# Last projection with the weights stationary, attention output in channel rows, and a new order of steps

## The chip, the cores and the metric

The kernel runs on one core of a Trainium2 chip. A core has a matrix engine (TensorE), three engines for elementwise work (VectorE, ScalarE, GpSimd), and SyncE, which here issues all DMAs. Each engine runs its own instruction list in order and waits on semaphores for the others. The metric is the device time of one execution in microseconds, median of several runs.

## The reference, cut to what matters

The input x has 4 sequences (batches) of 512 tokens with 256 channels. Two layers are computed, each followed by a residual addition and a layer norm.

```python
mixed = silu(causal_conv(x @ w_qkv, conv_w))     # 16 key heads, 32 value heads, 128 wide
q, k = l2norm(q) * 128 ** -0.5, l2norm(k)        # each key head serves two value heads
beta, g = sigmoid(x @ w_b), -exp(A_log) * softplus(x @ w_a + dt_bias)
def step(state, (q_t, k_t, v_t, g_t, b_t)):      # 512 tokens in sequence
    state = state * exp(g_t)
    delta = (v_t - k_t @ state) * b_t
    state = state + outer(k_t, delta)
    return state, q_t @ state
o = rmsnorm(o * silu(x @ w_z)) * norm_gamma      # per head
x = layernorm(x + o.reshape(..., 4096) @ w_out)  # the last projection of the attention
x = layernorm(x + moe(rmsnorm(x)))               # 8 experts, the top 2 of them weighed, and a shared one
```

All of it is float32.

## The kernel before

A body is one key head (two value heads) of one batch: 16 x 4 = 64 bodies. The recurrence is done in four chunks of 128 tokens, so a body has 8 cells (chunk x value head) of 128 x 128. In each cell a triangular matrix has to be inverted. That goes by doubling: six levels of `join` (a product with the blocks found so far), a mask on VectorE (`join` there, giving N), `growx` on TensorE, a copy to X on ScalarE (`growx` there), and a DMA that turns X into XT (`flip`). `growx` of a level needs the `flip` of the level before. After level 5, `newton`, `res`, `finish` and `tt` refine the inverse. The other steps of a body are: `proj` and `gate` (input projections, two or four matmuls each), `tap`, `conv`, `silu` (the convolution), `ktp`, `squares`, `kraw` (norms), `products`, `m`, `p`, `scan`, `diag` (decays and products of keys), then for the four chunks in sequence `read` (state times keys), `rhs`, `solve`, `u`, `write` and `s` (the new state, S), and `out`. `og` multiplies by the gate, `power`, `pow`, `ogs` norm the result.

The result then has to change its layout for the last projection: `ot` (L1386 to L1389) transposes 32 x 32 blocks on VectorE, `ost` (L871) writes them to DRAM and `old` (L838) loads them back as ogT with the channels on the partitions. `project` (L1156 to L1166) multiplies with wo, `acc` (L1400) adds the product to acc, which holds 128 token rows of 256 channels for each tile, over all heads. wo is w_out times gamma, scaled by GpSimd (`scale_wo`, L900 to L906) right behind `ogs`. `vt`, `vst`, `vld` do the same exchange of layout for v.

The order of all this is written out by hand in the table ORDER. Each engine has a list of (step, index, ahead); `rounds` runs it once per round k, for body k + ahead, so a round holds the work of four bodies at different ages. SP's list (L843 to L882) issues the DMAs: `flip`, `x0`, `vst`, `vld`, `ost`, `old`, `egs` and `ecs` (512 KB each, a row of decay factors spread over all partitions), and `weights`, once in four rounds (w_kh 768 KB, and wo_raw 256 KB, which waits for s_wog, that is for the scaling of the previous head's wo).

The expert layer runs at the end over four batches of 9 experts: `into` (L565) and `outof` (L581) on TensorE. For each batch `prepare_*` (L518 to L721) computes in numbered parts: part 0 adds acc to the rows of x (L670) and takes the statistics of the norm, part 2 normalises, parts 3 to 6 are the second norm, part 7 (L596) transposes, part 8 (L602) multiplies for the router, part 10 weighs. The parts of batch 0 stand in the functions `drain` of each engine, among the last bodies; those of batch 1 in part there, the rest between the experts.

Of the kernel before, what the change touches and what calls it, by code (L numbers as in the profile page):

```python
# [1494 lines left out]
```

## Time and profile before

| | us |
|---|---|
| three runs | 2419.18, 2420.91, 2423.63 |
| the profiled execution | 2420.51 |
| its span | 2418.8 |
| TensorE busy | 2197.0 |
| VectorE busy | 1900.1 |
| ScalarE, GpSimd busy | 1211.4, 1174.0 |

The span is the time from the first to the last instruction of the profiled execution. Busy time of TensorE is the sum over matmuls that overlap in a pipeline, so a stretch that is 100% busy can still be one in which matmuls start late; the distance between two starts is the better measure. An f32 matmul is two instructions in the records. In a timeline a row merges equal neighbours ("x8"), and what stands in brackets is the idle time ahead of it and who ended it.

### The profile page before, as it was taken

Reading aid. Unit: us, or ns where it says so; the run is one execution under the profiler, and the core shown is the slowest. Engines: PE = TensorE matmul, PEld = TensorE weight load, DVE = VectorE, ACT = ScalarE, POOL = GpSimd, SP = SyncE. Lnnn points to the kernel's source line nnn. Section 1 sums busy time; section 2 is a strip of 40 time slices with the busy share of each in tenths; the row PEclk is TensorE's granted clock in tenths of the full one; section 3 lists DMA queues with packets and bytes.
Section 4 is the critical chain, followed back from the end, with each engine's and each line's share of the span. In section 5 each row is a group of like instructions: output and inputs, shape, how many; then the busy total and the mean of one; then the engine's idle time right before and its main releaser. Section 6 shows DMA issues by size and latency. Waiting matters only on the chain.

```text
span 2418.8 us, 48563 instructions
## 1 busy us (share of the span) xinstructions
PE 2197.0 (91%) x16974; PEld 1709.1 (71%) x16974; DVE 1900.1 (79%) x3299; ACT 1211.4 (50%) x3805; POOL 1174.0 (49%) x1194
## 2 busy tenths in 40 slices
PE   6889999998999999998999999999998999978998
PEld 3677777776777777777777777777777777755565
DVE  4778888887888888787888888888888888864666
ACT  3555555554555555555555555555555555531210
POOL 2445555545554555554555545555554655531000
PEclk8999999999999999999999999999999999988999
DMA  3666767676767677577777676776767686662000
GB/s 117 156 146 159 177 151 164 148 167 153 165 149 162 153 161 173 145 167 149 166 158 171 141 166 152 166 171 156 165 142 166 158 176 145 147 151 69 27 9 18
DMA packets 597346, 349.88 MB, mean 145 GB/s; under 512 B 487665, under 2 KB 558705, under 8 KB 596849
## 3 DMA queue, kind: packets, MB, share of 16 engines
q1 hardware_dynamic: 597104, 346.78, 63.0%
q8 instruction: 137, 2.24, 0.4%
q14 instruction: 105, 0.85, 0.1%
HBM read 159.50 MB, written 69.73 MB: 95 GB/s over the span
## 4 chain that ended last, share of the span: by engine, by line
PE 46%; DMA 27%; DVE 13%; issue 5%; SPq 3%; ACT 2%; POOL 0%; POOLq 0%; DVEq 0%; ACTq 0%
DMA XT<-X 19%; PE bank L1034 9%; PE bank L1163 6%; DMA o_blocks<-og 6%; DVE og L1388 5%; PE bank L565 5%; PE bank L1053 4%; PE bank L1153 4%; DVE conv L1320 4%; PE bank L1087 3%; PE bank L1152 3%; PE bank L581 2%; SPq L838 2%; PE bank L1126 2%; DMA ogT<-o_blocks 2%
## 5 line engine op out<-in xcount | busy, mean ns | idle before, releaser
L1320 DVE SCALAR_TENSOR_TENSOR conv<-bank,cw_all,conv 128x511 f32<-128x511 f32 (+2 forms) x768 | 572.5, 746 | 20.6 <-ACT conv L1212 6.9
L1034 PE MATMUL bank<-xT,w_kh 128*128 128x512 f32 x1024 | 534.8, 614 | 1.6 <-ACT kraw L1241 1.1
L1265 ACT ACTIVATE X<-bank 128x512 f16<-128x512 f32 x384 | 228.6, 595 | 531.5 <-PE bank L1087 531.4
L1163 PE MATMUL bank<-wo,ogT 128*128 128x256 f32 x1024 | 287.3, 425 | 20.3 <-DMA ogT<-o_blocks 20.0
L987 POOL TENSOR_TENSOR ms<-ms,epsq 128x8 f32<-128x8 f32 x64 | 12.7, 198 | 584.8 <-ACT og L1278 584.8
L1163 PEld LDWEIGHTS bank<-wo,ogT 128*128 128x128 f32 x1024 | 256.6, 334 | 34.6 <-DMA ogT<-o_blocks 23.4
L1053 PE MATMUL bank<-w_kh,xT 128*128 128x256 f32 x1024 | 269.0, 396 | 4.7 <-DVE conv L1320 4.7
L1212 ACT ACTIVATE conv<-bank,cw_all 128x512 f32<-128x512 f32 x256 | 175.9, 687 | 162.1 <-PE bank L1034 162.1
L1077 PEld LDWEIGHTS bank<-X,mhiT 128*128 128x128 f16 x3072 | 145.6, 99 | 135.0 <-issue 75.4
L1087 PE MATMUL bank<-N,XT 128*128 128x64 f16 x2560 | 127.9, 193 | 119.8 <-DMA XT<-X 117.8
L1346 DVE TENSOR_TENSOR N<-bank,lev 128x512 f16<-128x512 f32 x320 | 218.0, 681 | 21.6 <-PE bank L1077 19.0
L1400 DVE TENSOR_TENSOR acc<-bank,acc 128x512 f32<-128x512 f32 x128 | 88.4, 692 | 182.2 <-PE bank L1163 182.2
L963 POOL TENSOR_SCALAR_AFFINE_SELECT mhiT<-m32T 128x512 f16<-128x512 f32 x128 | 78.8, 637 | 309.9 <-DVE m32T L1332 309.9
L1087 PEld LDWEIGHTS bank<-N,XT 128*128 128x128 f16 x2560 | 102.6, 98 | 153.3 <-issue 143.0
L1034 PEld LDWEIGHTS bank<-xT,w_kh 128*128 128x128 f32 x1024 | 170.2, 191 | 42.8 <-issue 31.6
L1053 PEld LDWEIGHTS bank<-w_kh,xT 128*128 128x128 f32 x1024 | 183.3, 194 | 23.4 <-DVE conv L1320 5.9
L1235 ACT ACTIVATE sqj<-bank 128x128 f16<-128x128 f32 x512 | 134.4, 277 | 124.8 <-PE bank L1044 124.8
L1153 PE MATMUL bank<-U,pT 128*128 128x128 f32 x1024 | 192.9, 280 | 0.0
L1136 PEld LDWEIGHTS bank<-U,keys 128*128 128x128 f32 x768 | 111.0, 192 | 83.2 <-ACT U L1270 65.1
L1356 DVE TENSOR_TENSOR TT<-bank,XT 128x512 f32<-128x512 f32 x128 | 82.5, 686 | 102.1 <-PE bank L1109 102.1
L1077 PE MATMUL bank<-X,mhiT 128*128 128x64 f16 x3072 | 154.8, 194 | 4.9 <-DMA X<-XT 2.9
L1152 PE MATMUL bank<-S,qE 128*128 128x128 f32 x768 | 153.6, 282 | 0.0
(176 smaller groups left out, 5088.0 us busy)
## 6 DMA issues: line engine op xcount, KB each, us to landing
egb<-rows SPq DMA_DIRECT2D x64, 512.0 KB, 4.7
ecb<-rows SPq DMA_DIRECT2D x64, 512.0 KB, 5.0
v_blocks<-conv SPq DMA_DIRECT2D x64, 512.0 KB, 3.0
vT<-v_blocks SPq DMA_DIRECT2D x256, 128.0 KB, 3.1
o_blocks<-og SPq DMA_DIRECT2D x64, 512.0 KB, 3.8
ogT<-o_blocks SPq DMA_DIRECT2D x256, 128.0 KB, 3.0
...
```

The source lines that it names most:

```text
L1034: mm = pe.matmul(PB[j % 2][:, :], w[:, k, g * P:(g + 1) * P], xT[:, k, b * SEQ:(b + 1) * SEQ], start=(k == 0), stop=(k == KT - 1))
L1053: mm = pe.matmul(PB[h][:, 256 * c:256 * c + 256], xT[:, k, t * P:(t + 1) * P], w[:, k, 512:768], start=(k == 0), stop=(k == KT - 1))
L1077: mm = pe.matmul(IB[p][:, x * 64:(x + 1) * 64], mhiT[:, p, x, :], blocks(X[:, p, x:x + 1, :], i, 0), start=True, stop=True)
L1087: mm = pe.matmul(IB[p][:, x * 64:(x + 1) * 64], XT[:, p, x, :], (last_N[:, x, :] if i == 5 else N[:, p, x, :]), start=True, stop=True)
L1152: pe.matmul(dst, qE[:, p, x, :], S[:, c, v * P:(v + 1) * P], start=True, stop=False)
L1153: mm = pe.matmul(dst, pT[:, p, x, :], U[:, x, :], start=(c == 0), stop=True)
L1163: mm = pe.matmul(OB[h][:, 256 * c:256 * c + 256], flat(ogT)[:, 2 * i + v::CELLS], wo[:, head % 2, v, :], start=(v == 0), stop=(v == VH - 1))
L1212: act.activation(conv[:, g, :], PB[i % 2][:, :], ACT.Copy, scale=cw_all[:, head, g * TAPS + 3:g * TAPS + 4]).then_inc(s_tap, 1)
L1235: act.activation(sqj[:, i, c, :], PB[i][:, c * P:(c + 1) * P], ACT.Square, accum_out=ssum[:, p, i, c:c + 1]).then_inc(s_sq, 1)
L1265: act.activation(blocks(X[:, p], i, 0), packed(IB[p], i), ACT.Copy).then_inc(s_x[p], 1)
L1320: dve.scalar_tensor_tensor(conv[:, g, m:], PB[j % 2][:, 0:SEQ - m], cw_all[:, head, g * TAPS + 3 - m:g * TAPS + 4 - m], conv[:, g, m:], op ...
L1346: dve.tensor_tensor(N[:, p].rearrange("p x (b s) -> p x b s", s=LEVELS[i]), packed(IB[p], i), blocks(lev[:, 1 + i:2 + i, :], i, 0).broadca ...
```

## The change

Four things change together.

The last projection: before, each of four chunks multiplied the tokens of a chunk (stationary, every eighth element) with wo (moving, 256 columns), for two value heads. Now wo is stationary (128 of its 256 output channels) and all 512 tokens of the body move, so that a body has four matmuls of 512 columns. The product has output channels on the partitions. acc is kept in this layout, 2 x 128 channel rows by 2048 tokens.

The exchange of layout: `ot` writes its blocks in the order that `vt` uses, and ogT is read in runs of 32 tokens.

The first norm: since acc is in channel rows, a new part 0 on TensorE transposes it by eight 128 x 128 blocks for each batch into two PSUM banks, and part 0 on VectorE adds x in two instructions from PSUM. For batch 0 the transposes stand behind `write` 1 of the last body but one; for the others ahead of or between the experts. Parts 0 and 2 of batch 1 on VectorE move from behind the last `ot` to behind the first expert steps.

The order: all five lists of ORDER are new.

```diff
 ORDER = {
     "tensor": [
-        ("join", 5, 1), ("out", 0, 0), ("solve", 3, 0), ("out", 1, 0), ("out", 2, 0), ("growx", 5, 1), ("out", 3, 0),
-        ("gate", 2, 2), ("join", 0, 2), ("newton", 0, 1), ("newton", 1, 1), ("growx", 0, 2), ("gate", 3, 2),
-        ("proj", 0, 3), ("join", 1, 2), ("finish", 0, 1), ("finish", 1, 1), ("proj", 1, 3), ("proj", 2, 3),
-        ("solve", 0, 1), ("growx", 1, 2), ("proj", 3, 3), ("write", 0, 1), ("products", 1, 2), ("join", 2, 2),
-        ("ktp", 0, 3), ("read", 1, 1), ("ktp", 1, 3), ("products", 0, 3), ("solve", 1, 1), ("growx", 2, 2),
-        ("write", 1, 1), ("proj", 4, 3), ("ktp", 2, 3), ("ktp", 3, 3), ("read", 2, 1), ("proj", 5, 3), ("join", 3, 2),
-        ("solve", 2, 1), ("proj", 6, 3), ("write", 2, 1), ("growx", 3, 2), ("proj", 7, 3), ("join", 4, 2),
-        ("gate", 0, 3), ("gate", 1, 3), ("read", 3, 1), ("project", 0, 0), ("project", 1, 0), ("growx", 4, 2),
-        ("project", 2, 0), ("project", 3, 0),
+        ("proj", 0, 3), ("join", 1, 2), ("finish", 0, 1), ("proj", 1, 3), ("finish", 1, 1), ("growx", 1, 2),
+        ("proj", 2, 3), ("solve", 0, 1), ("proj", 3, 3), ("write", 0, 1), ("join", 2, 2), ("read", 1, 1),
+        ("ktp", 0, 3), ("ktp", 1, 3), ("products", 1, 2), ("growx", 2, 2), ("solve", 1, 1), ("proj", 4, 3),
+        ("write", 1, 1), ("proj", 5, 3), ("join", 3, 2), ("ktp", 2, 3), ("read", 2, 1), ("ktp", 3, 3),
+        ("products", 0, 3), ("solve", 2, 1), ("growx", 3, 2), ("proj", 6, 3), ("write", 2, 1), ("join", 4, 2),
+        ("proj", 7, 3), ("gate", 0, 3), ("gate", 1, 3), ("project", 0, 0), ("growx", 4, 2), ("project", 1, 0),
+        ("project", 2, 0), ("join", 5, 2), ("project", 3, 0), ("read", 3, 1), ("out", 0, 1), ("out", 1, 1),
+        ("solve", 3, 1), ("out", 2, 1), ("growx", 5, 2), ("join", 0, 3), ("out", 3, 1), ("growx", 0, 3),
+        ("newton", 0, 2), ("newton", 1, 2), ("gate", 2, 3), ("gate", 3, 3),
     ],
     "vector": [
...
-        ("tt", 0, 2), ("tt", 1, 2), ("join", 1, 3), ("conv", 0, 4), ("conv", 1, 4), ("conv", 2, 4), ("s", 0, 2),
-        ("conv", 3, 4), ("conv", 4, 4), ("rhs", 1, 2), ("join", 2, 3), ("conv", 5, 4), ("ot", 0, 1), ("s", 1, 2),
...
+        ("join", 1, 2), ("tt", 0, 1), ("tt", 1, 1), ("conv", 0, 3), ("conv", 1, 3), ("conv", 2, 3), ("s", 0, 1),
+        ("join", 2, 2), ("conv", 3, 3), ("rhs", 1, 1), ("ot", 0, 0), ("conv", 4, 3), ("conv", 5, 3), ("p", 0, 2),
...
     "pool": [
-        ("diag", 0, 2), ("mhi", 0, 2), ("mhi", 1, 2), ("pairs", 0, 2), ("qe", 0, 1), ("pow", 0, 0), ("ogs", 0, 0),
-        ("ogs", 1, 0), ("keys", 0, 2), ("eq", 0, 2), ("mlo", 0, 2), ("kn", 0, 3),
+        ("pow", 0, 0), ("ogs", 0, 0), ("ogs", 1, 0), ("eq", 0, 2), ("kn", 0, 3), ("diag", 0, 3), ("mhi", 0, 3),
+        ("mhi", 1, 3), ("pairs", 0, 3), ("mlo", 0, 3), ("keys", 0, 3), ("qe", 0, 2),
     ],
     "sync": [
-        ("flip", 5, 1), ("flip", 0, 2), ("vst", 0, 2), ("flip", 1, 2), ("vld", 0, 2), ("egs", 0, 4), ("ost", 0, 0),
-        ("flip", 2, 2), ("old", 0, 0), ("ecs", 0, 3), ("flip", 3, 2), ("flip", 4, 2), ("x0", 0, 3), ("weights", 0, 2),
+        ("ecs", 0, 2), ("weights", 0, 4), ("flip", 1, 2), ("vld", 0, 2), ("ost", 0, 0), ("flip", 2, 2), ("egs", 0, 4),
+        ("old", 0, 0), ("flip", 3, 2), ("flip", 4, 2), ("x0", 0, 3), ("flip", 5, 2), ("flip", 0, 3), ("vst", 0, 3),
     ],
 }
...
-        acc = sb("acc", [P, TILES, D])
+        acc = sb("acc", [P, KT, TILES * P])
...
-        ogT4 = flat(ogT).rearrange("p (a k) -> p a k", a=Q32)
+        vn, ogT4 = quarters(vT), quarters(ogT)
...
         def prepare_tensor(pe, k, g):
+            if k == 0:
+                if g == 0:
+                    pe.wait_ge(s_zs, 2 * BODIES)
+                    pe.wait_ge(s_acc, 2 * (BODIES - B + 1))
+                elif g == 1:
+                    pe.wait_ge(s_acc, 2 * BODIES)
+                else:
+                    pe.wait_ge(s_rt, (g - 1) * RT + 1)
+                for c in range(CH):
+                    for t in range(KT):
+                        mm = pe.transpose(PICKS[g][c // 2][:, 256 * (c % 2) + P * t:256 * (c % 2) + P * (t + 1)],
+                                          acc[:, t, (g * CH + c) * P:(g * CH + c + 1) * P], ident)
+                mm.then_inc(s_atp, 1)
...
         def moe_tensor(pe):
+            prepare_tensor(pe, 0, 1)
             for i in range(DRAINED, B * NX):
...
+                if 0 < g < B - 1 and e == 0:
+                    prepare_tensor(pe, 0, g + 1)
...
         def prepare_vector(dve, k, g):
-                dve.tensor_tensor(xg[g], xg[g], acc[:, g * CH:(g + 1) * CH, :], ALU.add).then_inc(s_x1, 1)
+                dve.wait_ge(s_atp, g + 1)
+                for j in range(2):
+                    part = xg[g][:, 2 * j:2 * j + 2]
+                    dve.tensor_tensor(part, PICKS[g][j][:, :].rearrange("p (c n) -> p c n", c=2), part, ALU.add).then_inc(s_x1, 1)
...
                 elif name == "project":
-                    for v in range(VH):
-                        mm = pe.matmul(OB[h][:, 256 * c:256 * c + 256], flat(ogT)[:, 2 * i + v::CELLS], wo[:, head % 2, v, :],
-                                       start=(v == 0), stop=(v == VH - 1))
+                    mm = pe.matmul(OB[h][:, :], wo[:, head % 2, v, h * P:(h + 1) * P],
+                                   ogT4[:, :, v::VH].rearrange("p a c r -> p c a r"), start=(v == 0), stop=(v == VH - 1))
...
                 elif name == "ot":
-                    dve.transpose(flat(og2).rearrange("p (b s x) -> p b x s", b=Q32, x=CELLS),
+                    dve.transpose(flat(og2).rearrange("p (b x s) -> p b x s", b=Q32, s=32),
...
-                elif (name, i, n) == ("ot", 0, BODIES - 1):
-                    prepare_vector(dve, 0, 1)
-                    prepare_vector(dve, 2, 1)
```

ScalarE's list moves `growx` 0 ahead of `power` 0 and `zs`, `kraw` to right behind `squares` 0, and the copy for `join` 5 to behind `vals` and one `silu`.

## Rows read from the trace of the kernel before

**Rows 1.** The page's head and its part 1: busy time of each engine.
```profile
span 2418.8 us, 48563 instructions
...
PE 2197.0 (91%) x16974; PEld 1709.1 (71%) x16974; DVE 1900.1 (79%) x3299; ACT 1211.4 (50%) x3805; POOL 1174.0 (49%) x1194
```

**Rows 2.** The view by windows, 60 rounds: stretch, its length, busy times, granted clock.
```profile
112.32:2106.53 1994.21, 1840.73 (x15241) 1474.75 (x15240) 1647.92 (x2700) 1092.83 (x3482) 1080.65 (x1095) 1.00 0.71 159
```

**Rows 3.** Part 5 of the page, groups by line: busy, mean ns, idle before.
```profile
L1034 PE MATMUL bank<-xT,w_kh 128*128 128x512 f32 x1024 | 534.8, 614 | 1.6 <-ACT kraw L1241 1.1
...
L1163 PEld LDWEIGHTS bank<-wo,ogT 128*128 128x128 f32 x1024 | 256.6, 334 | 34.6 <-DMA ogT<-o_blocks 23.4
...
L1034 PEld LDWEIGHTS bank<-xT,w_kh 128*128 128x128 f32 x1024 | 170.2, 191 | 42.8 <-issue 31.6
```

**Rows 4.** Groups by line of TensorE over the whole span, the same columns.
```profile
L1077 PE MATMUL bank<-X,mhiT 128*128 128x64 f16 x3072 | 154.8, 194 | 4.9 <-DMA X<-XT 2.9 <-ACT X L1265 2.1
...
L1087 PE MATMUL bank<-N,XT 128*128 128x64 f16 x2560 | 127.9, 193 | 119.8 <-DMA XT<-X 117.8 <-DVE N L1346 1.6
```

**Rows 5.** TensorE's timeline of one round: start, length, step; L1087 is growx.
```profile
1202.99 2.27 PE L1163 MATMUL bank<-wo,ogT 128*128 128x256 f32 x8
1205.09 0.40 PE L1077 MATMUL bank<-X,mhiT 128*128 128x64 f16 x8
...
1208.09 0.40 PE L1087 MATMUL bank<-last_N,XT 128*128 128x64 f16 x8
...
1211.35 0.41 PE L1087 MATMUL bank<-N,XT 128*128 128x64 f16 x8
...
1214.08 1.94 PE L1034 MATMUL bank<-xT,w_kh 128*128 128x512 f32 x4
1215.85 0.61 PE L1126 MATMUL bank<-vals,TT 128*128 128x128 f32 x4
1216.30 0.40 PE L1087 MATMUL bank<-N,XT 128*128 128x64 f16 x8
...
1219.29 0.60 PE L1114 MATMUL bank<-S,kT 128*128 128x256 f32 x2
...
1221.28 0.40 PE L1087 MATMUL bank<-N,XT 128*128 128x64 f16 x8
...
1228.79 0.39 PE L1087 MATMUL bank<-N,XT 128*128 128x64 f16 x8 [0.93 <-DMA XT<-X]
...
1235.28 0.39 PE L1087 MATMUL bank<-N,XT 128*128 128x64 f16 x8 [0.78 <-DMA XT<-X]
```

**Rows 6.** VectorE's timeline of the same round: vt, the copy of S, ot.
```profile
1208.73 1.25 DVE L1392 STREAM_TRANSPOSE conv<-vT 128x1024 f32<-128x1024 f32 x1 [0.65 <-ACT vT L1226]
...
1218.15 0.48 DVE L1374 COPY S<-bank 128x128 f32<-128x128 f32 x2
...
1221.75 2.06 DVE L1388 STREAM_TRANSPOSE og<-og 128x1024 f32<-128x1024 f32 x1
```

**Rows 7.** SP's timeline of the same round: ost, flip 2, ecs, flip 3.
```profile
1223.84 0.34 SPq L871 DMA_DIRECT2D o_blocks<-og  x1
1224.22 1.96 SPq L856 DMA_TRANSPOSE XT<-X  x1
...
1229.40 0.43 SPq L841 DMA_DIRECT2D ecb<-rows  x1
1229.87 1.24 SPq L856 DMA_TRANSPOSE XT<-X  x1
```

**Rows 8.** GpSimd's timeline of the same round: the scaling of wo.
```profile
1217.63 1.04 POOL L905 TENSOR_TENSOR wo<-wo_raw,gam 128x512 f32<-128x512 f32 x1
```

**Rows 9.** Part 6 of the page, DMA issues: size, median us from issue to landing.
```profile
ecb<-rows SPq DMA_DIRECT2D x64, 512.0 KB, 5.0
```

**Rows 10.** TensorE's timeline in the tail: the last body's newton.
```profile
2176.70 0.27 PE L1099 MATMUL bank<-X,mhiT 128*128 128x128 f16 x1 [7.63 <-POOL mloT L971]
```

**Rows 11.** The chain that ended last, in order of time: the transposes of one batch.
```profile
2340.33 0.87 PE bank L596 x8
```

More of the change, by code:

```diff
@@ L46 @@
-        ("silu", 3, 2), ("growx", 5, 1), ("power", 0, 0), ("zs", 0, 2), ("growx", 0, 2), ("power", 1, 0),
-        ("zs", 1, 2), ("tap", 0, 3),
+        ("zs", 1, 1), ("tap", 0, 2), ("growx", 1, 1), ("u", 0, 0), ("tap", 1, 2), ("silu", 0, 2), ("squares", 0, 2),
+        ("kraw", 0, 2), ("growx", 2, 1), ("u", 1, 0), ("silu", 1, 2), ("tap", 2, 2), ("squares", 1, 2), ("u", 2, 0),
+        ("growx", 3, 1), ("tap", 3, 2), ("growx", 4, 1), ("vals", 0, 1), ("vals", 1, 1), ("silu", 2, 2),
+        ("join", 5, 1), ("u", 3, 0), ("silu", 3, 2), ("growx", 5, 1), ("growx", 0, 2), ("power", 0, 0), ("zs", 0, 2),
@@ L48 @@
+        ("power", 1, 0),
     ],
     "vector": [
-        ("m", 0, 3), ("m", 1, 3), ("acc", 0, 0), ("rhs", 3, 1), ("conv", 9, 3), ("acc", 1, 0), ("conv", 10, 3),
-        ("conv", 11, 3), ("og", 0, 1), ("vt", 0, 3), ("og", 1, 1), ("join", 0, 3), ("res", 0, 2), ("res", 1, 2),
-        ("tt", 0, 2), ("tt", 1, 2), ("join", 1, 3), ("conv", 0, 4), ("conv", 1, 4), ("conv", 2, 4), ("s", 0, 2),
-        ("conv", 3, 4), ("conv", 4, 4), ("rhs", 1, 2), ("join", 2, 3), ("conv", 5, 4), ("ot", 0, 1), ("s", 1, 2),
@@ L54 @@
-        ("p", 0, 3), ("rhs", 2, 2), ("p", 1, 3), ("join", 3, 3), ("conv", 6, 4), ("conv", 7, 4), ("conv", 8, 4),
-        ("s", 2, 2), ("scan", 0, 4), ("scan", 1, 4), ("join", 4, 3),
+        ("join", 1, 2), ("tt", 0, 1), ("tt", 1, 1), ("conv", 0, 3), ("conv", 1, 3), ("conv", 2, 3), ("s", 0, 1),
+        ("join", 2, 2), ("conv", 3, 3), ("rhs", 1, 1), ("ot", 0, 0), ("conv", 4, 3), ("conv", 5, 3), ("p", 0, 2),
+        ("s", 1, 1), ("p", 1, 2), ("join", 3, 2), ("rhs", 2, 1), ("conv", 6, 3), ("conv", 7, 3), ("scan", 0, 3),
@@ L56 @@
+        ("conv", 8, 3), ("m", 0, 3), ("scan", 1, 3), ("join", 4, 2), ("m", 1, 3), ("conv", 9, 3), ("conv", 10, 3),
+        ("s", 2, 1), ("acc", 0, 0), ("rhs", 3, 1), ("acc", 1, 0), ("conv", 11, 3), ("og", 0, 1), ("join", 0, 3),
+        ("vt", 0, 3), ("og", 1, 1), ("res", 0, 2), ("res", 1, 2),
     ],
     "pool": [
-        ("diag", 0, 2), ("mhi", 0, 2), ("mhi", 1, 2), ("pairs", 0, 2), ("qe", 0, 1), ("pow", 0, 0), ("ogs", 0, 0),
-        ("ogs", 1, 0), ("keys", 0, 2), ("eq", 0, 2), ("mlo", 0, 2), ("kn", 0, 3),
+        ("pow", 0, 0), ("ogs", 0, 0), ("ogs", 1, 0), ("eq", 0, 2), ("kn", 0, 3), ("diag", 0, 3), ("mhi", 0, 3),
@@ L238, in build_kernel @@
         s_xg = sem("s_xg")
+        s_atp = sem("s_atp")
         s_x1 = sem("s_x1")
@@ L503, in rows @@
                     sp.wait_ge(s_qe, BODIES - 1)
-                    sp.wait_ge(s_x1, 1)
+                    sp.wait_ge(s_x1, 2)
                 else:
@@ L761, in moe_vector @@
                     g, e = divmod(i, NX)
+                    if i == DRAINED:
+                        prepare_vector(dve, 0, 1)
+                        prepare_vector(dve, 2, 1)
                     if g + 1 < B:
@@ L892, in _ @@
             pool.memset(row_t[0][:, :, 0:1], 0.0).then_inc(s_rowz, 1)
-            pool.memset(acc[:, :, :], 0.0).then_inc(s_zero, 1)
+            pool.memset(flat(acc), 0.0).then_inc(s_zero, 1)
             for i, v in enumerate((0.5, -1.0)):
@@ L1396, in run @@
                     b = n % B
-                    a = acc[:, b * CH + 2 * i:b * CH + 2 * i + 2, :]
+                    a = acc[:, i, b * SEQ:(b + 1) * SEQ]
                     if n < B:
                         dve.wait_ge(s_zero, 1)
-                    dve.tensor_tensor(a, OB[i][:, :].rearrange("p (c n) -> p c n", c=2), a, ALU.add).then_inc(s_acc, 1)
+                    dve.tensor_tensor(a, OB[i][:, :], a, ALU.add).then_inc(s_acc, 1)
             def drain(name, i, n):
```

20 lines of the change are left out of this document (9 added, 11 removed).

## The prediction, made before the change was run

> **What bounds the kernel now.** I read the page's head and part 1 first: span 2418.8 us, TensorE busy 91% [rows 1]. The profiled execution took 2420.51 us, 1.7 more than its span and 0.4 under the median of 2420.91, so a change of the span carries over to the median one to one. The view by windows then shows the body loop: from the first full round to the last it takes 1994.21 us for 60 rounds, 33.24 us each, at a granted clock of 1.00, the 2.4 GHz level [rows 2]. Everything else is 425 us of start and tail. So the loop is the place.
>
> Busy TensorE is not full TensorE here. In the groups by line [rows 4] `growx` (L1087) is the one group with a large idle time ahead of it, 119.8 us, nearly all of it waiting for the DMA that turns X (`flip`). The TensorE timeline of one round [rows 5] shows where. I name the six growx steps of a body g0 to g5. Distances of starts: g5 to g0 3.26 us, g0 to g1 4.95, g1 to g2 4.98, g2 to g3 7.51, g3 to g4 6.49, and g4 to g5 5.33 (0.23 for g4 itself, then 1202.99 to 1208.09). A step's price is the distance to the next start in this timeline. With it the steps inside the first, second, third and last of these need 3.2, 4.9, 4.9 and 5.3 us, so TensorE is full there. The other two hold 5.35 and 5.7 us of work, and are long because flip 2 and flip 3 land late. In all 29.3 us of the mean round are work and 3.9 are stalls. This round has 32.5 us; the longer ones wait longer for the same two flips.
>
> Why flip 2 is late stands in SP's queue [rows 7]. SP issues in order, and `ost` stands ahead of flip 2 and waits for VectorE's transpose `ot`, which runs from 1221.75 to 1223.81 [rows 6]; so flip 2 goes out at 1224.22, 2.94 us after g2 starts, and g3 starts 4.57 us later. Flip 3 follows the 512 KB broadcast `ecs` at 1229.40 and g4 waits for it.
>
> **The projection.** Before: 8 matmuls of 256 columns with the tokens stationary, 16 instructions; eight start within 2.10 us, 4.20 us a round [rows 5]. After: 4 matmuls of 512 columns, 8 instructions of the form of L1034 [rows 3], four of which take 1.77 us (1214.08 to 1215.85), 3.54 us in all [rows 5]. Saved 0.66 us a round. The same columns are multiplied; what goes is half the loads. The old load takes 334 ns against 191 for one read in a row [rows 3], because its columns are 8 elements apart; the new one reads `wo` in a row. The new moving operand is read in runs of 32 elements. No row has that in f32. The nearest is `join` (L1077), whose moving f16 operand lies in runs of 2 to 64: 194 ns against 193 for growx with its operand in a row [rows 4]. So I price the runs at nothing. Upper end: the factor 334/191 on the whole matmul, 0.775 us each, 6.2 us a round, 2.0 more than now. A gain from the runs is excluded: L1034 reads in a row already.
>
> The Trainium skill ("SBUF — State Buffer", Door 1: The DMA port swizzle) says that SBUF serves accesses in 16-byte lines, so that f32 can be strided for free only within 4 elements. The trace agrees for the old load, 334 against 191 ns at a stride of 8. By that rule the runs of 32, eight full lines each, cost nothing either, and the sum stays; the upper end above would need a cost of another kind.
>
> **VectorE.** `ot` wrote with a stride of 8 and takes 2.06 us; it now has the form of `vt`, 1.25 us [rows 6]. That saves 0.8 us a round on VectorE, whose idle time is about 5 us in this round; alone it is worth nothing, but `ost` and flip 2 hang on it. `acc` keeps its shape. The four block loads keep their 1 KB runs: nothing.
>
> **The new order.** I walked the new lists through one round with the old durations. Steps between two growx change as follows (price per step: proj 0.885, project 0.885, gate 0.91, solve or write 0.45, read 0.44, products 0.90, newton pair 0.90, out 0.90, join 0.23).
> - g0 to g1: newton and gate 2 come in, proj 2 and solve 0 go out: 4.95+0.90+0.91-0.885-0.45 = 5.4 us. Flip 0 goes out about 1.1 after g0, behind flip 5, and needs some 4: hidden.
> - g1 to g2: proj 2 and solve 0 in, one products and solve 1 out: 4.97. Here is a new wait: read 1 now comes straight after write 0 and join 2, but needs VectorE's copy of S, which takes 0.48 us and starts some 0.2 after write 0 ends (the copy at 1218.15, the read at 1219.29 [rows 5, 6]); before, products hid it. Stall 0.5, so 5.5. Behind read 1 stand ktp, products, growx 2 and all later TensorE work, and on VectorE rhs 1 and then ot.
> - g2 to g3: 5.4 us of work, but flip 2 still decides. On VectorE `ot` moves ahead of conv 5 (0.7) and ends 0.8 sooner, against tt put in front: by my walk it ends about 1.8 after g2 instead of 2.5, and flip 2 goes out at about 2.2. The way from there to g3 was 4.57 in this round; `egs` no longer lies ahead, but the block loads of v are close. I keep 4.5: 6.7 us.
> - g3 to g4: proj 6, write 2 in, read 3 and half the project work out: 5.4 of work. `ecs` (5.0 us to land [rows 9]) is gone from ahead of flip 3, so its way should fall from the 6.49 seen to about 5.6.
> - g4 to g5: 6.3 of work, with read 3, project 3 and the first outs; nothing late.
> - g5 to g0: join 0 and the last out, 1.4; N must be ready 0.9 after join 0, just as long as VectorE needs (0.68 and the way). 1.5.
> Sum 31.0 us. What moved into the light work elsewhere: `ecs` now lies ahead of flip 1. Flip 1 goes out about 4 after ecs does and has 4 us to land, so in ordinary rounds I count 0.1: 31.1.
>
> Once in four rounds SP has `weights` ahead of flip 1. Its second DMA waits for the previous scaling of `wo` on GpSimd (L905, 1.04 us, right behind ogs, ending at 1218.67, 7.3 us after g0 [rows 5, 8]); in the old order this lay two rounds back, in the new one it is the scaling of the same round, while flip 1 would go out some 6.5 after g0. So flip 1, the loads of v and all that SP has behind them go out about 2 us later, and 1 MB more lies in the DMA queue ahead. TensorE waits about 3 us at g2, of which g2 to g3 gives 1 back, since ost is then ready earlier. 2 us in 4 rounds: 0.5 a round. The bounds are 0 and 1.2 (5 us in four).
>
> Round 31.6 against 33.24: 1.64 saved, 61 rounds, 100 us.
>
> **Start and tail.** GpSimd now makes mlo and keys a step earlier. In the tail TensorE stands 7.6 us at the last newton, waiting for mlo behind a norm step [rows 10]; that goes, and the flips or the X copy are late about 1 us instead: -6.5. Added: 32 transposes to turn the attention rows, 8 for each batch at 0.87 us like L596 [rows 11], 3.5 us, of which the last three batches lie on a TensorE that is full there; and the norm of batch 1 (4.6 us of VectorE) now stands between two experts instead of in VectorE's idle time, up to 2 us. The last project saves 0.7. Net -2, between -8 and +5. The start I leave at 0, plus or minus 5. Four batches of two PSUM additions instead of one SBUF addition: 0.2 us each, hidden.
>
> **Sum.** 2418.8 - 100 - 2 = 2317 for the span; with 1.7 around it 2318, and 0.4 more for the median of runs.
>
> **Rivals.**
> - TensorE alone decides. If both flips arrive in time, a round is 28.7 us of work and 0.8 of small waits, 29.5: 61 x 3.7 = 226 us less, 2193. For it: ot earlier, ecs away from flip 3. Against it: flip 2 still needs ot, ost and its own way after g2, 6.7 us against 5.4 of work.
> - The stalls only move. Then 0.66 us a round is left, less the 0.5 for weights or so: 10 to 40 us, 2380 to 2410. For it: ecs and weights now ahead of flip 1, and the read right behind the write. Against it: g2 to g3 loses its 0.7 on VectorE by rows.
> - Slower: the moving operand in runs costs what the strided load does. Each instruction 0.775 us, 2.0 us a round more than now; of the 1.64 above 0.98 are the order's, so the round is 34.3 and the time 2480. It decides from 0.65 us an instruction on ((4.20+0.98)/8), and if the stalls only move, from 0.53 (4.20/8). For it: the load at a stride of 8. Against it: the row of join.
> - Changed roles without effect (the loop does not feel it, within 0.2%, 5 us): hardly, the project work lies on a TensorE that is full in four of six gaps.
>
> **How the numbers follow.** Forecast 0.56; TensorE alone 0.15 (with the space between, 2200 to 2270); the stalls only move 0.19; no change 0.03; slower 0.07. 0.2% is about what a measurement of this kernel tells from no change. Faster 0.90, same 0.03, slower 0.07. The forecast's own range is 2275 to 2355; taking in half of each neighbour gives 2235 to 2385.
>
> **What would show it.** L1163 has 512 instructions, four starting within 1.77 us; three or more says that the runs cost. The transpose og<-og takes 1.25. g3 waits about 1.3 for flip 2, g4 at most 0.3. The S copy releases L1114 with about 0.5 at read 1. Every fourth round is 2 us longer, with g2 waiting for a flip behind w_kh. No wait for mloT of 7 us at the last newton. The forecast is wrong if the mean round is outside 31.0 to 32.3, above all if g2 waits in every round, which would mean that ecs ahead of flip 1 was underpriced.

## The result, and the profile after

| | before | after |
|---|---|---|
| median of four runs, us | 2420.05 | 2318.30 |
| lowest to highest | 2416.37 to 2423.63 | 2314.64 to 2323.43 |
| span of the profiled execution | 2418.8 | 2316.6 |

The ratio is 0.9581, 95% interval 0.9558 to 0.9605: 102 us faster. The forecast was 2318.

The page's head, its part 1 and two groups of its part 5 after the change (part 5: busy us, mean ns of one | idle before, releaser):

```profile
span 2316.6 us, 47612 instructions
...
PE 2153.8 (93%) x16494; PEld 1561.7 (67%) x16494; DVE 1843.2 (80%) x3303; ACT 1198.6 (52%) x3805; POOL 1224.3 (53%) x1194
...
L1184 PE MATMUL bank<-ogT,wo 128*128 128x512 f32 x512 | 268.3, 628 | 24.4 <-DMA ogT<-o_blocks 23.9
...
L1109 PE MATMUL bank<-N,XT 128*128 128x64 f16 x2560 | 127.7, 194 | 51.3 <-DMA XT<-X 49.1
```

TensorE's own work fell by 43 us [rows 1]. All its idle time, span less busy, fell from 221.8 [rows 1] to 162.8 us: 59 of the 102 us are stalls that went. The idle time ahead of `growx` (now L1109) fell from 119.8 [rows 4] to 51.3 us; other waits grew, as shown below. The view by windows over 60 rounds of the changed kernel (stretch, length, busy times, granted clock, DMA share, GB/s):

```profile
114.02:2006.52 1892.50, 1795.89 (x14761) 1333.07 (x14761) 1592.34 (x2700) 1080.80 (x3482) 1127.99 (x1095) 0.99 0.78 167
```

31.54 us a round against 33.24 [rows 2], so the loop gave 101.7 of the 102.2 us of span. The DMA share rose from 0.71 to 0.78. The same bytes in less time make about 0.75 of it; the rest is that the packets took some 4% longer in all.

TensorE's timeline of an ordinary round after (start, length, step):

```profile
1213.97 0.40 PE L1109 MATMUL bank<-N,XT 128*128 128x64 f16 x8
...
1219.86 0.40 PE L1109 MATMUL bank<-N,XT 128*128 128x64 f16 x8
...
1223.52 0.70 PE L1136 MATMUL bank<-S,kT 128*128 128x256 f32 x2 [0.35 <-DVE S L1397]
...
1225.39 0.40 PE L1109 MATMUL bank<-N,XT 128*128 128x64 f16 x8
...
1231.23 0.40 PE L1109 MATMUL bank<-N,XT 128*128 128x64 f16 x8
...
1236.95 0.40 PE L1109 MATMUL bank<-N,XT 128*128 128x64 f16 x8
1237.18 1.96 PE L1184 MATMUL bank<-ogT,wo 128*128 128x512 f32 x4
1238.98 0.40 PE L1099 MATMUL bank<-X,mhiT 128*128 128x64 f16 x8
...
1243.26 0.40 PE L1109 MATMUL bank<-last_N,XT 128*128 128x64 f16 x8
```

The growx rows (L1109) are g0 to g5. Four project instructions start within 1.80 us (1237.18 to 1238.98); before, eight took 2.10 [rows 5]. No growx waits for a flip here, and so it is in most ordinary rounds (those without `weights`): of the 41 between 250 and 2000 us, g3 waits in 14, for 0.21 us in the mean of all, and g4 in none. VectorE's and SP's timelines of the same round:

```profile
1225.15 1.23 DVE L1411 STREAM_TRANSPOSE og<-og 128x1024 f32<-128x1024 f32 x1
```

```profile
1226.42 0.34 SPq L893 DMA_DIRECT2D o_blocks<-og  x1
1226.84 1.51 SPq L878 DMA_TRANSPOSE XT<-X  x1
1228.39 0.77 SPq L863 DMA_DIRECT2D egb<-rows  x1
```

`ot` takes 1.23 instead of 2.06 us [rows 6] and starts before g2. Flip 2 goes out at 1226.84, 1.45 us after g2 instead of 2.94 [rows 5, 7]. g3 starts 4.39 us behind it, but no longer because of it: TensorE's own steps fill the gap.

Every fourth round, with `weights`, looks different. SP, GpSimd and TensorE in such a round:

```profile
1153.18 0.43 SPq L863 DMA_DIRECT2D ecb<-rows  x1
1153.71 0.77 SPq L841 DMA_DIRECT2D w_kh<-w_heads  x1
1159.05 0.33 SPq L844 DMA_DIRECT2D wo_raw<-w_out  x1
1159.42 1.24 SPq L878 DMA_TRANSPOSE XT<-X  x1
```

```profile
1157.98 1.04 POOL L927 TENSOR_TENSOR wo<-wo_raw,gam 128x512 f32<-128x512 f32 x1
```

```profile
1155.43 0.40 PE L1109 MATMUL bank<-N,XT 128*128 128x64 f16 x8
1163.38 0.39 PE L1109 MATMUL bank<-N,XT 128*128 128x64 f16 x8 [2.25 <-DMA XT<-X]
...
1164.20 1.92 PE L1056 MATMUL bank<-xT,w_kh 128*128 128x512 f32 x2
```

SP stands at wo_raw from 1154.5 until the scaling of wo ends at 1159.02; flip 1 goes out behind it, and g2 comes 7.95 us after g1 instead of 5.53. Rounds of this kind take 33.7 us in the mean (32.6 to 34.7), the others 30.9 (29.9 to 31.9).

The stall at g2 has a second price. The two `proj` instructions at 1164.20 take 1.71 us to the next start, where two take 0.93 in the ordinary round above. The view by windows of the stall and of what follows it (columns as above, the granted clock is the third number from the end):

```profile
1161.00:1163.40 2.40, 0.15 (x3) 0.05 (x2) 2.36 (x4) 0.90 (x5) 1.82 (x2) 1.00 1.18 263
1163.60:1167.30 3.70, 3.70 (x17) 2.47 (x14) 0.67 (x3) 1.50 (x3) 0.33 (x2) 0.56 1.13 292
```

TensorE did 0.15 us of work in 2.40 us, and then the granted clock is 0.56 in the mean of 3.70 us, so most of that is at the 1.2 GHz level. That happens behind g2 in 10 of the 13 rounds of this kind and in no ordinary round. Those 10 take 33.9 us, the other three 32.7.

### The profile page after: what moved, and what is told of

Read it like the earlier page. It is cut to its first block and busy times, and to the rows that moved or that the text cites. A ratio compares the mean times of both kernels' runs of the same rounds, so it can differ in the third digit from the quotient of the medians.

```text
span 2316.6 us, 47612 instructions
## 1 busy us (share of the span) xinstructions
PE 2153.8 (93%) x16494; PEld 1561.7 (67%) x16494; DVE 1843.2 (80%) x3303; ACT 1198.6 (52%) x3805; POOL 1224.3 (53%) x1194
## 5 line engine op out<-in xcount | busy, mean ns | idle before, releaser
L1056 PE MATMUL bank<-xT,w_kh 128*128 128x512 f32 x1024 | 559.6, 630 | 10.6 <-ACT kraw L1264 10.1
L1184 PE MATMUL bank<-ogT,wo 128*128 128x512 f32 x512 | 268.3, 628 | 24.4 <-DMA ogT<-o_blocks 23.9
L985 POOL TENSOR_SCALAR_AFFINE_SELECT mhiT<-m32T 128x512 f16<-128x512 f32 x128 | 131.2, 1025 | 255.6 <-DVE m32T L1355 255.6
L1075 PE MATMUL bank<-w_kh,xT 128*128 128x256 f32 x1024 | 248.9, 386 | 0.4 <-DVE conv L1343 0.4
L1099 PEld LDWEIGHTS bank<-X,mhiT 128*128 128x128 f16 x3072 | 139.9, 98 | 122.4 <-issue 110.5
L1387 DVE SCALAR_TENSOR_TENSOR rhs<-bank,sc_all,vals 128x128 f32<-128x128 f32 x384 | 116.0, 344 | 108.2 <-PE bank L1136 108.2
L1293 ACT ACTIVATE U<-bank 128x256 f32<-128x256 f32 x256 | 99.9, 390 | 181.7 <-PE bank L1148 181.6
L963 POOL TENSOR_TENSOR decb<-tri_sb,bfac 128x1024 f32<-128x1024 f32 x64 | 121.4, 1896 | 126.1 <-DVE pT L1363 126.1
L1158 PEld LDWEIGHTS bank<-U,keys 128*128 128x128 f32 x768 | 121.1, 200 | 97.8 <-ACT U L1293 66.3
L1056 PEld LDWEIGHTS bank<-xT,w_kh 128*128 128x128 f32 x1024 | 163.2, 196 | 27.0 <-issue 18.7
L1109 PE MATMUL bank<-N,XT 128*128 128x64 f16 x2560 | 127.7, 194 | 51.3 <-DMA XT<-X 49.1
L1109 PEld LDWEIGHTS bank<-N,XT 128*128 128x128 f16 x2560 | 108.3, 98 | 98.1 <-issue 84.0
L1099 PE MATMUL bank<-X,mhiT 128*128 128x64 f16 x3072 | 154.3, 193 | 8.6 <-DMA X<-XT 7.2
L1175 PEld LDWEIGHTS bank<-U,pT 128*128 128x128 f32 x1024 | 155.2, 192 | 3.7 <-issue 0.5
L1349 DVE TENSOR_TENSOR_SCAN decb<-egb,decb 128x512 f32<-128x512 f32 x128 | 155.5, 1215 | 0.0
```

The lines of the kernel that those rows point to most:

```text
L1056: mm = pe.matmul(PB[j % 2][:, :], w[:, k, g * P:(g + 1) * P], xT[:, k, b * SEQ:(b + 1) * SEQ], start=(k == 0), stop=(k == KT - 1))
L1075: mm = pe.matmul(PB[h][:, 256 * c:256 * c + 256], xT[:, k, t * P:(t + 1) * P], w[:, k, 512:768], start=(k == 0), stop=(k == KT - 1))
L1099: mm = pe.matmul(IB[p][:, x * 64:(x + 1) * 64], mhiT[:, p, x, :], blocks(X[:, p, x:x + 1, :], i, 0), start=True, stop=True)
L1109: mm = pe.matmul(IB[p][:, x * 64:(x + 1) * 64], XT[:, p, x, :], (last_N[:, x, :] if i == 5 else N[:, p, x, :]), start=True, stop=True)
L1175: mm = pe.matmul(dst, pT[:, p, x, :], U[:, x, :], start=(c == 0), stop=True)
L1184: mm = pe.matmul(OB[h][:, :], wo[:, head % 2, v, h * P:(h + 1) * P], ogT4[:, :, v::VH].rearrange("p a c r -> p c a r"), start=(v == 0), st ...
```

## The experiments

All gaps below are mean distances in us between starts of growx, worked out from TensorE's timelines over 48 to 56 rounds between 250 and 2000 us, of one execution each; a kernel stands here with the ratio of its runs to those of the kernel before on the same chip. The chips differ: the kernel before took 2425.36 us beside e1 to e4, 2405.47 beside e5 to e8 and 2420.55 beside e9 to e12. So kernels of different groups are compared by ratio and by round, not by their times.

| kernel | g0-g1 | g1-g2 | g2-g3 | g3-g4 | g4-g5 | g5-g0 | round | ratio |
|---|---|---|---|---|---|---|---|---|
| before | 5.03 | 5.04 | 7.73 | 6.75 | 5.41 | 3.26 | 33.22 | 1 |
| after | 5.53 | 6.17 | 6.26 | 5.82 | 6.31 | 1.45 | 31.54 | 0.958 |
| e1 order alone | 5.46 | 6.25 | 6.61 | 6.04 | 6.81 | 1.45 | 32.61 | 0.981 |
| e2 projection alone | 5.29 | 4.99 | 7.51 | 6.86 | 5.02 | 3.26 | 32.94 | 0.994 |
| e3 weights late | 5.60 | 5.54 | 6.15 | 6.10 | 6.32 | 1.44 | 31.15 | 0.944 |
| e4 wo_raw late | 5.51 | 5.99 | 6.08 | 5.93 | 6.35 | 1.44 | 31.29 | 0.953 |
| e5 e2, egs later | 5.30 | 5.00 | 7.01 | 7.22 | 5.02 | 3.26 | 32.81 | 0.998 |
| e6 old ot | 5.52 | 6.15 | 6.55 | 6.02 | 6.32 | 1.45 | 32.00 | 0.977 |
| e7 moving stride 8 | 5.48 | 6.17 | 6.58 | 6.97 | 9.23 | 1.44 | 35.87 | 1.082 |
| e8 ecs ahead of flip 3 | 5.50 | 6.07 | 6.16 | 7.35 | 6.59 | 1.45 | 33.12 | 1.006 |
| e9 e3, egs behind flip 4 | 5.75 | 5.59 | 6.09 | 5.42 | 6.32 | 2.73 | 31.89 | 0.965 |
| e10 e2, ecs behind flip 4 | 5.74 | 5.01 | 7.57 | 5.71 | 5.03 | 4.27 | 33.32 | 1.005 |
| e11 e3, read 1 later | 5.54 | 5.77 | 6.13 | 6.14 | 6.32 | 1.44 | 31.33 | 0.952 |
| e12 e9 and e11 | 5.76 | 5.78 | 6.12 | 5.38 | 6.32 | 2.74 | 32.09 | 0.969 |

**The two halves.** e1 is the kernel before with only the five lists of ORDER new. e2 is the changed kernel with only the lists of before.

> The old projection, the old transpose and the old norm, with the new order alone. Theory (layout and order both give, and ot must be short for the new order): the project steps are 0.66 us a round longer again and ot ends 0.8 us later ahead of flip 2, so a round is 30.8+0.66+0.6 = 32.1 us and every fourth 3 us longer, 32.9 in the mean: about 2400 us, 1% under the kernel before. Rival 1 (the order is worth nothing by itself): 2420. Rival 2 (the order is nearly the whole gain): 2360 or less, that is only the 0.66 us a round of the projection missing.

> The new projection, transpose and norm, with the old order. Theory: 0.66 us a round from the projection and 0.5 to 0.6 from ot, which lets flip 2 go sooner, 32.0 us a round; the wait for mlo in the tail stays and 3.5 us of transposes come on top: about 2350 us. Rival 1 (the gain is the layout's): 2320. Rival 2 (the stalls only move): 0.66 us a round, 2380.

Measured: e1 2376.65 us, ratio 0.9812 (0.978 to 0.9843), between the theory (2400) and the rival for which the order is nearly the whole gain (2360). e2 2408.46, 0.9937 (0.9912 to 0.9962): a clear miss, far less than expected. By rounds the order alone gives 0.61 us and the projection alone 0.28, together 1.68: 0.8 us a round comes only from having both. In e2 the 0.66 us of work left g3-g4 and g4-g5, but only the 0.39 at g4-g5 shows, ot's earlier end gives 0.22 at g2-g3 for 0.8 on VectorE, and g0-g1 and g3-g4 take 0.26 and 0.11 back. SP's timeline of e2:

```profile
1233.32 0.43 SPq L863 DMA_DIRECT2D egb<-rows  x1
1235.62 0.34 SPq L893 DMA_DIRECT2D o_blocks<-og  x1
1236.00 1.72 SPq L878 DMA_TRANSPOSE XT<-X  x1
```

and TensorE's, g2 and g3:

```profile
1233.88 0.40 PE L1109 MATMUL bank<-N,XT 128*128 128x64 f16 x8
1242.19 0.39 PE L1109 MATMUL bank<-N,XT 128*128 128x64 f16 x8 [2.21 <-DMA XT<-X]
```

Flip 2 goes out 2.12 us after g2, 0.8 sooner than before [rows 5, 7], but g3 now starts 6.19 us later, not 4.57. This round is a long one; in the mean of the ordinary rounds flip 2 lands 5.26 us after its issue in e2 and 4.75 before. The 512 KB of egs went out 2.7 us ahead of it instead of 3.5. The next run tests that reading.

**e5**, e2 with egs behind flip 2:

```diff
-("vld", 0, 2), ("egs", 0, 4), ("ost", 0, 0), ("flip", 2, 2), ("old", 0, 0),
+("vld", 0, 2), ("ost", 0, 0), ("flip", 2, 2), ("egs", 0, 4), ("old", 0, 0),
```

> The kernel of e2 (new projection, old order), with one DMA moved: egs (512 KB) goes from ahead of ost to behind flip 2. In e2 flip 2 went out 0.8 us sooner than before, yet g2 to g3 fell only from 7.73 to 7.51 us. Theory (the queue: flip 2 lies behind egs and ost, 1 MB, so going out sooner only makes it wait there): g2 to g3 falls by 0.8 to 1.2 us, g3 to g4 may rise by 0.3 since egs now lies nearer to flip 3: about 32.2 us a round against e2's 32.9, 40 us less than e2, ratio to the kernel before about 0.975. Rival (flip 2 takes what it takes, the egs ahead of it does not matter): no change to e2, ratio 0.992 to 0.996.

Measured: 2397.43 us, 0.9977 (0.9959 to 0.9995). The place was right and the total wrong: g2-g3 fell by 0.5, with flip 2 landing after 4.74 us instead of 5.26, and g3-g4 rose by 0.36. By rounds e5 is 0.13 us shorter than e2, by ratio 0.4% longer; on two chips that tells no difference. Its waits of TensorE between 300 and 2000 us (total, times, longest), and those of e2:

```profile
PE bank L1109 <- DMA XT<-X: 67.6, 78, 2.1
PE bank L1184 <- DMA ogT<-o_blocks: 49.8, 46, 2.4
```

```profile
PE bank L1109 <- DMA XT<-X: 122.5, 95, 3.2
...
PE bank L1184 <- DMA ogT<-o_blocks: 5.4, 9, 0.9
```

The wait for flips nearly halved, and the loads of ogT, now behind the same 512 KB, took it over.

**The weights.** e3 moves `weights` from ahead of flip 1 to behind x0; e4 leaves the 768 KB of w_kh and moves only wo_raw, the one that waits for the scaling.

```diff
-("ecs", 0, 2), ("weights", 0, 4), ("flip", 1, 2),
+("ecs", 0, 2), ("flip", 1, 2),
...
-("flip", 4, 2), ("x0", 0, 3), ("flip", 5, 2),
+("flip", 4, 2), ("x0", 0, 3), ("weights", 0, 2), ("flip", 5, 2),
```

> The changed kernel with weights moved back in SP's list, from ahead of flip 1 to behind x0 (ahead of flip 5), two rounds later. Theory (flip 1 is late once in four rounds because weights stands ahead of it): the 15 long rounds lose their 3.2 us, at most 0.5 comes back at flip 5 or flip 0: 2270 to 2280 us. Rival (the long rounds come from 1 MB of transfer, wherever it is put): the rounds stay long at another place, 2310 to 2320.

> As the changed kernel, but of the two DMAs of weights only the second (wo_raw, 256 KB, the one that waits for the scaling) goes behind x0; the 768 KB of w_kh stay ahead of flip 1. Theory (it is mostly the wait for the scaling, 2.3 us of issue time for flip 1): the long rounds lose 2 to 2.5 us, 2280 to 2290. Rival (the bytes ahead of flip 1 in the DMA queue): the long rounds keep 2 to 3 us, 2305 to 2318.

Measured: e3 2292.31 us, 0.9443 (0.9414 to 0.9472); its rounds with weights take 31.2 us in the mean like the others (32.4 is the longest of all), and the clock never fell between 250 and 2000 us. But its ordinary rounds are 0.27 us longer than those of the changed kernel, mostly in the wait for ogT (29.0 us between 300 and 2000 for 14.8). e4 2305.02, 0.9526 (0.9485 to 0.9567); its rounds with weights take 32.3.

A round with weights took 2.8 us more than an ordinary one in the changed kernel, and the rounds of e3 and e4 split that into three parts of about equal size. In e4, in the 10 of 13 such rounds in which the clock did not fall, it is 0.9: flip 1 goes out 1.2 us after g1 as in any round, but lands after 6.2 instead of 3.4 us, behind the 768 KB of w_kh. In the changed kernel, in the three in which the clock did not fall (no more stand for this), it is 1.9: the other 0.9 or so are the wait for the scaling, with the 256 KB of wo_raw, which make flip 1 go out 3.95 us after g1. The rest, 1.2 us in 10 rounds of 13, is the clock. e3 is the fastest kernel of the study, and the clock is a large part of why: it stood at the lower level for 34.1 us of the loop in the changed kernel and for none in e3.

**e6 and e7, the exchange of layout.** e6 is the changed kernel with the old form of `ot`, which writes with a stride of 8; the blocks of attention output then reach the product in another order. e7 adds a moving operand read at a stride of 8, so that they are in the right one again.

```diff
-dve.transpose(flat(og2).rearrange("p (b x s) -> p b x s", b=Q32, s=32),
+dve.transpose(flat(og2).rearrange("p (b s x) -> p b x s", b=Q32, x=CELLS),
...
-               ogT4[:, :, v::VH].rearrange("p a c r -> p c a r"), start=...
+               flat(ogT).rearrange("p (t c v) -> p v c t", c=CH, v=VH)[:, v], start=...
```

> The changed kernel with the old form of ot alone (written with a stride of 8, 2.06 instead of 1.24 us; the attention output then reaches the last projection in a permuted order, the amount of work is the same). Theory (in the new order flip 2 has a short way, so ot, ost, flip 2, g3 is a chain in which 0.8 us count): g2 to g3 rises by 0.4 to 0.8 us, 25 to 45 us more than the changed kernel, ratio to the kernel before 0.968 to 0.976. Rival (ot has slack in the new order as it had none to give in e2): within 5 us of the changed kernel, ratio 0.958.

> The changed kernel with the old form of ot and the moving operand of the projection read as ot then leaves it, every eighth f32 element; the result is the reference's. Beside e6 it tells what a stride of 8 costs a moving operand. Theory A (nothing or little, since a moving column has twice the time of a stationary one): four instructions start within 1.8 us, the time of e6. Theory B (the same 2.6 ns a column as the strided load, 334 ns for 128): 1.33 us an instruction, 10.7 us of projection a round instead of 3.5, about 7 us a round and 400 us more than e6.

Measured: e6 2347.6 us, 0.9771 (0.9738 to 0.9803), as expected in size: 0.8 us more on VectorE cost 0.46 us a round (31.54 to 32.00). In ordinary rounds it is 0.76, of that 0.53 at g2-g3 and 0.25 at g3-g4; the rounds with weights are 0.5 shorter than in the changed kernel, since the clock falls in 6 of 13 and not in 10. But the way is not the one that the text gives, by ost and flip 2 to g3: g3 waits for the flip less than in the changed kernel, 0.06 us for 0.21. The waits of ScalarE between 300 and 2000 us for `conv`, which stands behind ot in VectorE's list, first in the changed kernel, then in e6, and one of TensorE's loads that only e6 has:

```profile
ACT qT L1249 <- DVE conv L1343: 31.7, 42, 0.8
```

```profile
ACT qT L1249 <- DVE conv L1343: 59.3, 41, 1.5
...
PEld bank L1066 <- ACT qT L1249: 9.5, 41, 0.2
```

So the longer ot makes conv late, conv makes the copy to qT late, and `ktp` 2 (L1066 on qT) starts 0.28 us later behind `join` 3 in the mean of the ordinary rounds; the steps behind it add the rest. The part at g3-g4 fits the way by ost: the first project waits longer for ogT, 0.52 us for 0.31. e7 2598.43, 1.0817 (1.0776 to 1.0857), between the two theories of its text. Its matmuls, by source line (duration min/median/max), and four of them in its timeline:

```profile
L1184 PEld LDWEIGHTS bank<-ogT,wo x512: 186/192/337, 133.2 to 2399.7; 128*128 128x128 f32 x171
L1184 PE MATMUL bank<-ogT,wo x512: 1077/1098/1264, 133.2 to 2400.6; 128*128 128x512 f32 x171
```

```profile
1210.15 3.89 PE L1184 MATMUL bank<-ogT,wo 128*128 128x512 f32 x4
```

In the changed kernel the same median is 592 ns. So a stride of 8 makes the record of such an instruction 1.85 times as long, and the distance of two starts about twice as long (0.93 us for 0.45; the next step begins 3.71 us after 1210.15); the eight instructions cost 3.9 us a round more than in e6. The runs of 32 of the change cost nothing against a row: the median of `proj` (L1056), which reads a row, is 592 ns too in the loop of the same trace.

**The places of the broadcasts.** e8 is the changed kernel with ecs back between old and flip 3; e10 is e2 with ecs behind flip 4; e9 is e3 with egs behind flip 4.

```diff
# e8
-("ecs", 0, 2), ("weights", 0, 4), ("flip", 1, 2),
+("weights", 0, 4), ("flip", 1, 2),
-("old", 0, 0), ("flip", 3, 2),
+("old", 0, 0), ("ecs", 0, 3), ("flip", 3, 2),
# e10
-("old", 0, 0), ("ecs", 0, 3), ("flip", 3, 2), ("flip", 4, 2), ("x0", 0, 3),
+("old", 0, 0), ("flip", 3, 2), ("flip", 4, 2), ("ecs", 0, 3), ("x0", 0, 3),
# e9
-("flip", 2, 2), ("egs", 0, 4), ("old", 0, 0), ("flip", 3, 2), ("flip", 4, 2),
+("flip", 2, 2), ("old", 0, 0), ("flip", 3, 2), ("flip", 4, 2), ("egs", 0, 4),
```

> The changed kernel with ecs (512 KB) back at its old place in SP's list, between old and flip 3. Theory (ecs ahead of flip 3 makes it late, ecs ahead of flip 1 costs nothing in ordinary rounds): g3 to g4 rises from 5.82 to 6.5 us or more, ordinary g1 to g2 stays at 5.53, and the long rounds lose some 0.5: 35 us more than the changed kernel, ratio 0.972. Rival (the place of ecs is indifferent, what flip 3 loses flip 1 wins): ratio 0.955 to 0.961.

> New projection in the order of before (2408 us, 0.9937 of before), with one step moved: ecs stands behind flip 4 instead of ahead of flip 3. Queue theory: the new projection gained only 15 us alone because flip 3 stood behind 512 KB; without that g3 to g4 falls from 6.86 to about 6.0 us, the round from 32.9 to about 32.0, the time is 2345 to 2360, ratio about 0.973. Rival, the order gains only as a whole (TensorE's and VectorE's lists decide): g3 to g4 stays above 6.6 or g4 to g5 takes it back, time 2390 or more, ratio over 0.988.

> The changed kernel with weights behind x0 (2292 us, 0.944 of before) and, besides, the 512 KB of egs behind flip 4 instead of between flip 2 and the loads of ogT. Queue theory: the wait of project for ogT (29.0 us between 300 and 2000 us with weights late, landing of the loads 4 us) comes from the 512 KB ahead of them and goes, so TensorE wins up to 25 us: 2268 us, ratio 0.935. Rival, the bytes only move: egs is then in the way of x0, weights and flip 5, a growx or a proj waits there instead, and the time is 2285 to 2300, ratio 0.942 to 0.948.

Measured: e8 2415.64 us, 1.0055 (1.003 to 1.008). One DMA of 512 KB in another place costs 1.6 us a round, nearly all that the change gives. A small part comes by the clock, which stood at the lower level for 54.6 us of e8's loop against 34.1. e10 2429.94, 1.0053 (1.0027 to 1.0079), slower than e2. e9 2340.51, 0.9651 (0.9617 to 0.9685), slower than e3. Waits of TensorE between 300 and 2000 us in e8, e10 and e9:

```profile
PE bank L1109 <- DMA XT<-X: 86.7, 76, 2.7
PE bank L1184 <- DMA ogT<-o_blocks: 29.3, 34, 2.3
```

```profile
PE bank L1109 <- DMA XT<-X: 74.4, 51, 2.7
PE bank L1099 <- DMA X<-XT: 42.7, 50, 2.4
```

```profile
PE bank L1099 <- DMA X<-XT: 59.8, 54, 1.9
```

Both expectations of a gain missed for one reason. In e10 g3-g4 fell from 6.86 to 5.71, more than forecast; in e9 g3-g4 fell from 6.10 to 5.42, and the wait for ogT (29.0 us in e3) left the list. But x0, the DMA that brings the next X, now stands right behind 512 KB, and `join` 0 (L1099), which in e2 and e3 never was in the list, waits for it: g5-g0 rose by 1.0 and 1.3 us. SP and TensorE in e9:

```profile
1229.72 0.58 SPq L863 DMA_DIRECT2D egb<-rows  x1
1230.40 1.24 SPq L884 DMA_TRANSPOSE X<-XT  x1
```

```profile
1235.41 0.41 PE L1099 MATMUL bank<-X,mhiT 128*128 128x64 f16 x8 [1.31 <-DMA X<-XT]
```

5.0 us from issue to use; x0 lands after 4.8 us in the median of e9, after 3.1 in e3. In e10 g0-g1 rose too (5.29 to 5.74), and all of it in the rounds behind `weights`: there g0-g1 is 7.84 us, with 2.15 of wait of `finish` for flip 5, which SP issues behind ecs, x0 and weights; in the others it is 5.06. In e2 the two are 6.14 and 5.00, and in e9 they are 6.99 and 5.37.

**e11 and e12.** e11 is e3 with read 1 behind both `ktp`; e12 is e11 with e9's edit as well.

```diff
-("join", 2, 2), ("read", 1, 1), ("ktp", 0, 3), ("ktp", 1, 3), ("products", 1, 2),
+("join", 2, 2), ("ktp", 0, 3), ("ktp", 1, 3), ("read", 1, 1), ("products", 1, 2),
```

> The changed kernel with weights behind x0, and read 1 behind both ktp instead of straight behind write 0 and join 2. If the wait of read 1 for the copy of S (0.35 us a round, 19.2 us between 300 and 2000) is on the path, g1 to g2 falls from 5.5 to about 5.2 and the time to about 2273 us, ratio 0.936. Rival, the chain behind the read decides: read 1 starts 0.5 us later, so rhs 1, ot and flip 2 are later, g2 to g3 takes the 0.35 back, and the time stays at 2290 to 2300, ratio 0.943 to 0.948.

> All three moves on the changed kernel: weights behind x0, egs behind flip 4, read 1 behind ktp. If both single moves win and are independent: 2250 us, ratio 0.927. If both only move the wait: about 2292 us, ratio 0.944. If egs wins because the loads of ogT were late and read 1 gives it back at flip 2: 2270.

Measured: e11 2306.35 us, 0.9518 (0.9485 to 0.9552), slower than e3, which neither text said. The wait of the read for S left the list, and another took its place, of `ktp` for ScalarE:

```profile
PE bank L1066 <- ACT kT L1249: 34.0, 55, 0.6
```

34.0 us for 19.2. e12 2348.95, 0.9691 (0.9659 to 0.9724), the losses of both.

## Why the prediction came out right, step by step

**Projection.** Forecast 3.54 us a round for eight instructions, measured 3.60. That the runs of 32 cost nothing held (592 ns, like `proj`). The slower rival had its cause right for a stride that the change doesn't have: e7 is slower than before, with 0.93 us an instruction where the rival decided at 0.65. The load fell from 334 to 191 ns as said (median 191 in the changed kernel, 192 in e7's row, which reads wo alike).

**ot and flip 2.** This is the step whose mechanism did not hold. The transpose has the forecast's length. I put its end 1.8 us after g2 and flip 2 out at 2.2, "flip 2 still decides" with g3 waiting 1.3 us for it, and so 6.7 us. In ordinary rounds ot ends at 1.0, flip 2 goes out at 1.45 and lands 4.26 us later, about as priced, and g3 waits 0.21. So the flip is out of the way in two rounds of three. What fills the gap, 6.11 us, is TensorE's work, which I had at 5.4 without waits: the larger part of the difference is that `proj` 4 starts 0.85 us after `solve` 1 where my price was 0.45; it waits there for ScalarE's `kraw`, which the sum does not have. Another 0.2 is the flip. The number for g2-g3, 6.7 for 6.26 in the mean, is 0.44 too high. With the old ot, e6 and e1 have ot's end at 1.8 and flip 2 out at 2.2, just where I had put them for the new one: my walk came to ot 0.8 us too late.

**The other gaps** (forecast, measured mean): g0-g1 5.4, 5.53; g1-g2 in an ordinary round 5.5, 5.53, with the wait of read 1 for S at 0.35 instead of 0.5; g3-g4 5.6, 5.82; g4-g5 6.3, 6.31; g5-g0 1.5, 1.45. The excess of g3-g4 has a wait that I had not named: the first project now waits for ogT, whose landing rose from 3.0 to 4.3 us because egs went out just ahead (3.0 again in e9). It cost 14.8 us between 300 and 2000, 8.2 before. Ordinary rounds had 31.1 forecast and 30.9 measured.

**weights.** The place is the one forecast. The size was 0.5 us a round and measured 0.7, 2.8 us in every fourth round instead of 2. I had 3 us of wait at g2, of which g2-g3 gives 1 back. g1-g2 rose by 2.7 us, but g2-g3 gave nothing back: it rose from 6.11 to 6.76 us. The term that the sum lacks is the clock behind the stall. In the three rounds in which the clock did not fall, g2-g3 is 5.79 and the round 1.9 us longer than an ordinary one, the forecast's 2. I had also named 1 MB in the queue without a price; e4 shows that w_kh's bytes alone are 0.9 us. w_kh took 7.4 us to land, 4.6 in e3.

**The sum** for a round was 31.6 and is 31.54: -0.2 in ordinary rounds and +0.2 for weights cancel, and within the ordinary round -0.6 at g2-g3 stands against +0.3 at g3-g4 and +0.2 at g0-g1. That is luck in a picture that had the places right, but neither what ends g2-g3 nor the clock, and the total alone would not show it.

**Start and tail.** Forecast 0 and -2, measured +1.7 (the first full round begins at 114.02 for 112.32) and -2.2. The parts of the tail: the wait for mlo went, as said; TensorE's timeline after has

```profile
2047.25 1.04 PE L596 MATMUL bank<-tri_sb,acc 128*128 128x128 f32 x8
2053.41 1.23 PE L1148 MATMUL bank<-rhs,TT 128*128 128x128 f32 x4 [4.38 <-DVE rhs L1387]
...
2067.02 0.23 PE L1121 MATMUL bank<-X,mhiT 128*128 128x128 f16 x1 [0.45 <-ACT X L1288]
...
2120.50 6.72 PE L1184 MATMUL bank<-ogT,wo 128*128 128x512 f32 x8 [9.04 <-DMA ogT<-o_blocks]
```

0.45 us ahead of the last newton instead of 7.63 [rows 10]. But a solve waits 4.38 for VectorE, which norms first, and the last project takes 6.72 us (6.11 before, at sixteen instructions), where the sum had let it save 0.7. In both kernels TensorE stood over 9 us ahead of it and the granted clock was low during it (0.62 and 0.54). Right in total, not in its terms; no run took the tail apart.

**What the prediction didn't say.** It added the projection's gain and the order's as if they were independent. e1, e2 and e6 show that they aren't: of the 1.68 us a round 0.8 need both. The early end of ot is worth 0.46 in the new order (e6), by conv and by ogT, and 0.22 at g2-g3 in the old (e2), where g3 waits for flip 2 in every round. Had only one half been made, this way of adding would have missed. "The stalls only move" was given 0.19 and is wrong for this change, but it is what e2, e5, e9, e10 and e11 each did. "TensorE alone decides" stays out: even e3 has 31.15 us against 29.5. Its condition, both flips in time, is nearly met in ordinary rounds; what keeps them at 30.9 is in the main the small waits that are left, 1.1 us together: S 0.35, ogT 0.31, flips 0.3, kraw 0.16.

Open: what makes the start 1.7 us longer, and why the clock fell behind 10 of 13 stalls at g2 and not behind the other three. Nor was the order taken apart beyond single places in SP's list and one in TensorE's: what the new lists of VectorE, ScalarE and GpSimd give is not shown.
